# Sum-and-route stage with the shared expert: expert by batches with its weights stationary, positions behind each batch's logits

## The chip, the cores and the metric

The kernel is one launch on one NeuronCore of a Trainium2 chip. The metric is device time in microseconds (us), from the first to the last instruction of the core. TensorE (PE in the rows, PEld for its weight loads) multiplies, VectorE (DVE) and ScalarE (ACT) work element by element, GpSimd (POOL) issues the scatters by index, SyncE (SP) issues the other DMAs. Each engine runs its own list of instructions in order and waits for the others by semaphores.

## The reference

Four layers, each an attention or mixture (cond) and a feed-forward (ffn), on x of 4 batches of 512 tokens of 256 values, all in float32:

```python
x = x + _L0_ffn_ref(_L0_cond_ref(x, ...), ...)
x = x + _L1_ffn_ref(_L1_cond_ref(x, ...), ...)
x = x + _L2_ffn_ref(_L2_cond_ref(x, ...), ...)
x = x + _L3_ffn_ref(_L3_cond_ref(x, ...), ...)
```

The change lies where layer 1 ends and layer 2 begins. Layer 1 ends with a sum of two experts' rows per token; `_L2_cond_ref` is a mixture of 8 experts, of which each token takes two, plus one shared expert that all tokens take:

```python
logits = (logits_h + logits_g / GE_TEMP) / (1.0 + 1.0 / GE_TEMP)
topk_w, topk_idx = jax.lax.top_k(jax.nn.softmax(logits, axis=-1), K)   # K = 2 of E = 8
...
y = (y_sel * topk_w[..., None]).sum(1).reshape(b, s, h)
p = _leaky(hidden_states @ sw_gate) * (hidden_states @ sw_up) @ sw_down
y = y + p
```

`sw_gate`, `sw_up` and `sw_down` are 256x256 each; `_leaky` is max(x, 0.01 x).

## The kernel before

The program is a chain of stages (`stage`, line 89), each a block in which the five engines run their own lists, with a barrier between blocks: a stage starts when every engine has finished the one before. The stage of this case is `combine_and_share` (line 2312). Tokens lie 128 to a tile, 4 tiles to a batch, 16 tiles in all. Three things share the stage, each an object whose methods are called engine by engine, in an order written out by hand:

- `Combine` (`com`, L2216): VectorE adds the two weighted expert rows of a batch to `all_x`, eight instructions for a batch.
- `Router` (`part`): `tensor_turn` transposes the batch (L1655), ScalarE copies it to `all_xt` (L1620), `tensor` multiplies by the router's weights (L1670, L1674), `vector_ahead` takes the two largest of 8 logits for each token (L1717 to L1743), `tensor_after` counts with 0/1 matmuls how many earlier tokens chose each expert (L1687 to L1692, in bf16), `vector` makes the positions from these ranks (L1755 to L1761), and GpSimd scatters the batch's 8 tiles of rows, four of `all_x` and four of a copy (`scalar_double`, L1631), to the positions (L1605). `vector_last` (L1768 to L1799) makes the table of tiles and the routing weights. When all scatters have landed and the table is there, SyncE reads the table and loads the first tiles of sorted rows for the next stage (`first_rows`, L2006).
- `SharedExpert` (`shx`): tile by tile, in a pipeline. For tile t, `tensor(pe, t)` multiplies the tile (as the stationary side) with gate and up weights side by side (L2261, two matmuls of 512 columns into `gu_ps`), transposes the hidden values of tile t-1 (L2269, two), and multiplies those of tile t-2 with the down weights (L2277, two of 256 columns). ScalarE copies the gate half (L2286), the transposed hidden values (L2291) and the product to `all_h` (L2295); VectorE makes the leaky value (L2304) and the product with up (L2309).

The trace holds two records for each float32 matmul, so that "x4" beside L2261 is the two matmuls of one tile. After `part.tensor_after(pe, 3)` the PE list holds only the shared expert's tiles 7 to 15 and the two steps of tail; on VectorE `vector_last` stands behind tile 10.

Of the kernel before, what the change touches and what calls it, by code (L numbers as in the profile page):

```python
# [2231 lines left out]
class SharedExpert:  # L2232
# [6 lines left out]
    def __init__(self, nc, c, weights, com, stack):  # L2239
        m = Memory(nc, stack, "shx")  # L2240
        self.nc, self.c, self.com = nc, c, com
        self.wgu, self.wd, self.loaded = weights.wgu, weights.wd, weights.loaded
        self.act, self.lin, self.hid = ([m.sb(f"{x}{n}", [P, D]) for n in range(2)] for x in ("act", "lin", "hid"))
        self.hid_t = [m.sb(f"hid_t{n}", [P, KD, P]) for n in range(2)]
        self.gu_ps = [m.ps(f"gu_ps{n}", [P, 2, D]) for n in range(2)]
        self.t_ps = m.ps("t_ps", [P, KD, P])
        self.y_ps = m.ps("y_ps", [P, D])
        names = "gu_ready act_ready lin_ready hid_ready ht_ready ht_copied y_ready h_ready".split()
        (self.gu_ready, self.act_ready, self.lin_ready, self.hid_ready, self.ht_ready, self.ht_copied, self.y_ready,
         self.h_ready) = (m.sem(x) for x in names)  # L2250

    def tensor(self, pe, t):

        nc = self.nc
        if t == 0:
            pe.wait_ge(self.loaded, 48)
        if t < NT:
            if t >= 2:
                pe.wait_ge(self.hid_ready, t - 1)
            for k in range(KD):  # L2260
                last = nc.tensor.matmul(self.gu_ps[t % 2][:], self.c.xt[:, k, P * t:P * (t + 1)], self.wgu[:, k, :, :], start=(k == 0), stop=(k == KD - 1))  # L2261
            last.then_inc(self.gu_ready, 1)
        if 1 <= t <= NT:
            v = t - 1
            pe.wait_ge(self.hid_ready, v + 1)
            if v >= 1:
                pe.wait_ge(self.ht_copied, v)
            for f in range(KD):
                last = nc.tensor.transpose(self.t_ps[:, f, :], self.hid[v % 2][:, P * f:P * (f + 1)], self.c.ident[:])  # L2269
            last.then_inc(self.ht_ready, 1)  # L2270
        if t >= 2:
            v = t - 2
            pe.wait_ge(self.ht_copied, v + 1)
            if v >= 1:
                pe.wait_ge(self.h_ready, v)
            for f in range(KD):
                last = nc.tensor.matmul(self.y_ps[:], self.hid_t[v % 2][:, f, :], self.wd[:, f, :], start=(f == 0), stop=(f == KD - 1))  # L2277
            last.then_inc(self.y_ready, 1)

    def scalar(self, a, t):  # L2280
        nc = self.nc
        if t < NT:
            a.wait_ge(self.gu_ready, t + 1)
            if t >= 2:
                a.wait_ge(self.lin_ready, t - 1)
            nc.scalar.activation(self.act[t % 2][:], self.gu_ps[t % 2][:, 0, :], ACT.Copy).then_inc(self.act_ready, 1)  # L2286
        if 1 <= t <= NT:
            a.wait_ge(self.ht_ready, t)
            if t >= 3:
                a.wait_ge(self.y_ready, t - 2)  # L2290
            nc.scalar.activation(self.hid_t[(t - 1) % 2][:], self.t_ps[:], ACT.Copy).then_inc(self.ht_copied, 1)  # L2291
        if t >= 2:
            a.wait_ge(self.y_ready, t - 1)
            a.wait_ge(self.com.added, QT * ((t - 2) // QT + 1))
            nc.scalar.activation(self.c.h[:, t - 2, :], self.y_ps[:], ACT.Copy).then_inc(self.h_ready, 1)  # L2295

    def vector(self, dve, t):
        nc = self.nc
        if t < NT:
            n = t % 2  # L2300
# [388 lines left out]
```

## Time and profile before

| | us |
|---|---|
| median of three runs | 2277.09 (2274.95 to 2286.39) |
| the profiled execution | 2278.94 |
| its span on the core | 2277.1 |
| the stage: first to last instruction | 1157.86 to 1254.01 |

Busy time in the whole span: PE 2005.0 us (88%), DVE 1112.2 us (49%), ACT 988.5 us (43%), POOL 559.8 us (25%). The stage takes 96 of 2277 us. All rows below are of the profiled execution and count from its start. In a timeline row stand the start, the time taken, engine, line, operation and operands, the count, and in brackets how long the engine had been idle and what ended that; "remote" and "issue" mean that no instruction of another engine was found that the engine was waiting for at that moment. PEclk is the granted clock of TensorE, 1.00 for 2.4 GHz and 0.50 for 1.2 GHz.

### The profile page before, as it was taken

What the parts mean: (1) busy time and instruction counts of PE and PEld (TensorE: products, weight loads), DVE (VectorE), ACT (ScalarE), POOL (GpSimd) and SP (SyncE); (2) the same over time, 40 slices, a digit from 0 to 9 for tenths busy, and PEclk for the clock granted to TensorE, in tenths of its full rate; (3) what the DMA queues carried; (4) which work ended last, traced back from release to release, by engine and by line L of the source; (5) the groups of instructions that cost most, each with busy time, mean ns of one, the idle gap of its engine ahead of it and who ended that gap; (6) DMA issues with size and microseconds to landing.
All of it is one profiled execution on the core that took longest, in us unless ns stands there. A gap on an engine that the chain in (4) does not pass through costs nothing. (4 is left out here: it accounts for less than half of the span.)

```text
span 2277.1 us, 44630 instructions
## 1 busy us (share of the span) xinstructions
PE 2005.0 (88%) x15891; PEld 1415.1 (62%) x15891; DVE 1112.2 (49%) x3378; ACT 988.5 (43%) x2602; POOL 559.8 (25%) x872
## 2 busy tenths in 40 slices
PE   6899999897999996999967865996989999969994
PEld 3477777654777775566644544883567776736663
DVE  5388882275888824000043336006678883331113
ACT  2388881155888811111112231223678883212221
POOL 2022220065111115211123333115711111421111
PEclk9999999998999998999978986998989999979997
DMA  2185523001633121433131541741010004131113
GB/s 84 38 247 154 147 78 97 0 1 53 174 109 104 35 77 45 143 103 104 55 100 62 170 151 48 231 142 42 1 50 21 21 12 149 45 126 45 46 42 122
DMA packets 156826, 197.80 MB, mean 87 GB/s; under 512 B 15251, under 2 KB 129902, under 8 KB 156620
## 3 DMA queue, kind: packets, MB, share of 16 engines
q1 hardware_dynamic: 145004, 168.83, 24.6%
q0 software_dynamic: 11616, 26.26, 3.2%
q8 instruction: 124, 2.03, 0.4%
q14 instruction: 82, 0.67, 0.1%
HBM read 120.33 MB, written 88.64 MB: 92 GB/s over the span
## 5 line engine op out<-in xcount | busy, mean ns | idle before, releaser
L995 ACT ACTIVATE att_pr<-all_h,att_nmax 128x128 f32<-128x128 f32 (+3 forms) x768 | 420.8, 551 | 49.1 <-DVE att_nmax L948 49.1
L1059 PEld LDWEIGHTS att_t_ps<-all_ident,att_pr 64*128 64x128 f32 x3840 | 163.0, 139 | 104.0 <-issue 48.4
L1059 PE MATMUL att_t_ps<-all_ident,att_pr 64*128 64x64 f32 x3840 | 170.0, 223 | 10.4 <-DVE att_pt L957 10.3
L1255 PE MATMUL out_y_ps<-outw_wo,mem_qt 128*128 128x256 f32 x768 | 178.7, 386 | 0.0
L1918 PE MATMUL exp_f_h_ps<-exp_f_xs_t,cw_f_w 128*128 128x512 f32 (+1 forms) x512 | 172.7, 497 | 1.5 <-DVE exp_f_xs_t L1955 1.5
L1930 PE MATMUL exp_f_y_ps<-cw_f_w,exp_f_hid 128*128 128x256 f32 x768 | 168.4, 379 | 0.0
L957 DVE COPY att_pt<-att_t_ps 128x1024 f32<-128x1024 f32 (+2 forms) x168 | 166.7, 992 | 0.0
L1255 PEld LDWEIGHTS out_y_ps<-outw_wo,mem_qt 128*128 128x128 f32 x768 | 144.5, 193 | 24.7 <-issue 6.2
L1985 ACT ACTIVATE exp_f_hid<-exp_f_h_ps 128x512 f32<-128x512 f32 (+1 forms) x128 | 62.4, 490 | 219.3 <-PE exp_f_h_ps L1918 216.4
L1930 PEld LDWEIGHTS exp_f_y_ps<-cw_f_w,exp_f_hid 128*128 128x128 f32 x768 | 144.8, 190 | 19.5 <-issue 0.5
L995 ACT ACTIVATION_READ_ACCUMULATOR att_pr<-all_h,att_nmax 128x1 f32 x768 | 145.5, 189 | 0.0
L948 DVE CUSTOM_DVE_ANT_0 all_h<-att_s_ps,att_bias,mem3k_nsn 128x128 f32<-128x128 f32 (+3 forms) x256 | 128.2, 548 | 35.1 <-PE att_s_ps L1042 27.3
L948 DVE CUSTOM_DVE_ANT_0 all_h<-att_s_ps,att_bias,mem1k_nsn 128x128 f32<-128x128 f32 (+3 forms) x256 | 128.3, 549 | 34.8 <-PE att_s_ps L1042 26.2
L2100 PE MATMUL til_f_ab_ps<-tw_f_wab,til_f_xs_t 128*128 x312 | 143.4, 603 | 1.4 <-DVE til_f_xs_t L2161 1.4
L948 DVE CUSTOM_DVE_ANT_0 all_h<-att_s_ps,att_bias,mem0k_nsn 128x128 f32<-128x128 f32 (+3 forms) x256 | 127.9, 547 | 33.4 <-PE att_s_ps L1042 26.9
L1918 PEld LDWEIGHTS exp_f_h_ps<-exp_f_xs_t,cw_f_w 128*128 128x128 f32 x512 | 99.7, 195 | 68.8 <-issue 61.1
L915 POOL COPY att_rexp<-att_rinv 128x512 f32<-128x512 f32 x96 | 58.6, 610 | 336.5 <-DVE att_rinv L961 336.5
L1007 ACT ACTIVATE att_pt<-att_t_ps 128x1024 f32<-128x1024 f32 (+1 forms) x120 | 112.7, 939 | 39.9 <-PE att_t_ps L1059 35.7
L113 POOL TENSOR_TENSOR in_qn<-in_qn,all_minus_half 128x16 f32<-128x16 f32 x32 | 113.9, 3562 | 37.4 <-DVE in_qn L529 37.2
L730 PE MATMUL in_q_ps<-inw_wq,all_xt 128*128 128x512 f32 x256 | 119.9, 614 | 2.8 <-ACT all_xt L627 2.8
L1897 POOL DMA_INDIRECT expert_f<-exp_f_ys,exp_f_idx x48 | 46.7, 972 | 304.5 <-DVE exp_f_ys L1964 254.5
L2161 DVE COPY til_f_xs_t<-til_f_x_ps 128x256 f32<-128x256 f32 x39 | 16.6, 425 | 186.3 <-PE til_f_x_ps L2087 186.3
(395 smaller groups left out, 3661.6 us busy)
## 6 DMA issues: line engine op xcount, KB each, us to landing
sorted_c<-all_zero SPq DMA_DIRECT2D x8, 2056.0 KB, 14.1
sorted_f<-all_zero SPq DMA_DIRECT2D x8, 2056.0 KB, 11.8
cw_f_w<-in_L_ffn_w_dram SPq DMA_DIRECT2D x16, 1024.0 KB, 8.1
cw_f_w<-in_L_ffn_W_dram SPq DMA_DIRECT2D x16, 1024.0 KB, 7.0
band<-rev SPq DMA_DIRECT2D x2, 4096.0 KB, 19.3
att_bias<-band SPq DMA_DIRECT2D x32, 256.0 KB, 3.0
com_f_rows<-expert_f SPq DMA_DIRECT2D x16, 512.0 KB, 5.9
tw_f_wab<-in_L_ffn_w_dram SPq DMA_DIRECT2D x2, 4096.0 KB, 20.0
```

Source lines behind the costliest of these rows:

```text
L113: pool.tensor_tensor(value, value, c.minus_half[0:value.shape[0], 0:1].to_broadcast(list(value.shape)), ALU.pow).then_inc(ready, 1)
L730: last = nc.tensor.matmul(q_ps[t % 2][:, n, :], c.xt[:, k, P * t:P * (t + 1)], wq[:, k, S * n:S * (n + 1)], start=(k == 0), stop=(k == KD ...
L948: nc.vector.tensor_tensor_reduce(sc[u % 4][:, hh, at], s_ps[(2 * u + hh) % 3][:, at], bias_ap(i, q, hh), -1.0, c.nsn[:, b + k, q, h:h + 1] ...
L957: nc.vector.tensor_copy(*pt_and_turned(u)).then_inc(t_copied[e % 2], 1)
L995: nc.scalar.activation(pr[u % 4][:, hh, at], sc[u % 4][:, hh, at], ACT.Exp, scale=-1.0, bias=nmax[:, b + k, q, h:h + 1], accum_out=rsum[:, ...
L1007: nc.scalar.activation(*pt_and_turned(u), ACT.Copy).then_inc(t_copied[e % 2], 1)
L1059: last = nc.tensor.transpose(t_ps[e % 2][:, half, (q + 1) * (n * hh + k) + kb, :], pr[u % 4][d, hh, at:at + P], c.ident[d, d])
L1255: nc.tensor.matmul(y_ps[b % 2][:, q, :], c.out_t[:, p, P * at:P * (at + 1)], wo[:, p, :], start=(p == 0), stop=False)
L1918: last = nc.tensor.matmul(h_ps[f % 4][:, 0:cap], w1_sb[n][:, k, P * f:P * (f + 1)], xs_t[n][:, k, :], start=(k == 0), stop=(k == KD - 1))
L1930: last = nc.tensor.matmul(y_ps[(YT * n + t // 2) % 2][:, t % 2, :], hid[n][:, f, P * t:P * (t + 1)], w2_sb[n][:, f, :], start=(f == 0), st ...
L1985: nc.scalar.activation(hid[n][:, f, :], h_ps[f % 4][:, 0:cap], func).then_inc(hid_ready, 1)
L2100: last = nc.tensor.matmul(ab_ps[t % 2][:, n, :], xs_t[t % 2][:, k, :], tw.wab[:].rearrange("p (e k) n f -> p k n e f", k=KD)[:, k, n, at, ...
```

## The change

The router's and the combine's own instructions stay as they are; their places in the lists change. The shared expert is computed by batches of 512 tokens. The weights are now the stationary side and the tokens the moving one, so that the hidden values come out transposed, as the down product wants them: `tensor_gate(b, f)` makes half f of the hidden values of batch b, gate and up, in four matmuls of 512 columns; ScalarE copies the gate part and VectorE makes the two products, each on 512 columns; `tensor_out(b)` does the down product of the four tiles in eight matmuls of 256 columns, and `scalar_out` copies it to `all_h` in two pieces. The transposes (L2269) and their copies (L2291) are gone. Gate halves and outputs take turns in two PSUM buffers of two banks each.

```diff
-            for k in range(KD):
-                last = nc.tensor.matmul(self.gu_ps[t % 2][:], self.c.xt[:, k, P * t:P * (t + 1)], self.wgu[:, k, :, :], start=(k == 0), stop=(k == KD - 1))
...
-            for f in range(KD):
-                last = nc.tensor.transpose(self.t_ps[:, f, :], self.hid[v % 2][:, P * f:P * (f + 1)], self.c.ident[:])
...
+    def gate_bank(self, b, f):
+        return self.bank[(3 * b + f) % 2]
+    def out_bank(self, b):
+        return self.bank[(3 * b + 2) % 2].ap().rearrange("p a (t d) -> p a t d", d=D)
+    def tensor_gate(self, pe, b, f):
...
+        if b and f == 0:
+            pe.wait_ge(self.hid_ready, 2 * b)
+        if b and f == 1:
+            pe.wait_ge(self.h_ready, 2 * b)
+        for n in range(2):
             for k in range(KD):
+                last = nc.tensor.matmul(self.gate_bank(b, f)[:, n, :], self.wgu[:, k, n, P * f:P * (f + 1)], self.c.xt[:, k, S * b:S * (b + 1)],
+                                        start=(k == 0), stop=(k == KD - 1))
+        last.then_inc(self.gu_ready, 1)
+    def tensor_out(self, pe, b):
...
+        pe.wait_ge(self.hid_ready, 2 * b + 2)
+        for a in range(2):
+            for t in range(2):
+                tok = slice(P * (2 * a + t), P * (2 * a + t + 1))
+                for f in range(KD):
+                    last = nc.tensor.matmul(self.out_bank(b)[:, a, t, :], self.hid[b % 2][:, f, tok], self.wd[:, f, :], start=(f == 0), stop=(f == KD - 1))
             last.then_inc(self.y_ready, 1)
...
+    def scalar_gate(self, a, b, f):
...
+        self.nc.scalar.activation(self.act[n % 2][:], self.gate_bank(b, f)[:, 0, :], ACT.Copy).then_inc(self.act_ready, 1)
+    def scalar_out(self, a, b):
...
+            a.wait_ge(self.y_ready, 2 * b + n + 1)
+            self.nc.scalar.activation(self.c.h[:, QT * b + 2 * n:QT * b + 2 * n + 2, :], self.out_bank(b)[:, n, :, :], ACT.Copy).then_inc(self.h_ready, 1)
...
+        nc.vector.tensor_tensor(self.hid[b % 2][:, f, :], self.lin[n % 2][:], self.gate_bank(b, f)[:, 1, :], ALU.mult).then_inc(self.hid_ready, 1)
...
     @block.vector
     def _(dve):
         com.vector(dve, 0)
         com.vector(dve, 1)
         part.vector_ahead(dve, 0)
+        part.vector(dve, 0)
+        shx.vector_gate(dve, 0, 0)
         com.vector(dve, 2)
-        shx.vector(dve, 0)
-        part.vector(dve, 0)
         part.vector_ahead(dve, 1)
-        shx.vector(dve, 1)
+        part.vector(dve, 1)
+        shx.vector_gate(dve, 0, 1)
         com.vector(dve, 3)
...
         part.vector(dve, 3)
...
+        shx.vector_gate(dve, 2, 0)
+        shx.vector_gate(dve, 2, 1)
+        part.vector_last(dve)
+        shx.vector_gate(dve, 3, 0)
+        shx.vector_gate(dve, 3, 1)
```

On TensorE at the stage's start, from behind batch 1's transposes (before) and from batch 1's transposes (now); `turn_c` and `route_c` are the router's tiles, `shx` the shared expert's. Before:

```order
L1670 MATMUL turn_c_l_ps<-rw_c_wg_t,rw_c_g_t 128x32
L1674 MATMUL turn_c_l_ps<-rw_c_wr,all_xt 128x8 x8
L2261 MATMUL shx_gu_ps<-shw_wgu,all_xt 128x512 x2
L1687 MATMUL turn_c_r_ps<-route_c_sel,all_before 128x32
```

Now:

```order
L1655 MATMUL turn_c_x_ps<-all_ident,all_x 128x128 x8
L2268 MATMUL shx_bank<-all_xt,shw_wgu 128x512 x4
L1687 MATMUL turn_c_r_ps<-route_c_sel,all_before 128x32
L1692 MATMUL turn_c_r_ps<-route_c_sel,all_ones_b 128x24
L1692 MATMUL turn_c_r_ps<-route_c_sel,all_ones_b 128x16
L1692 MATMUL turn_c_r_ps<-route_c_sel,all_ones_b 128x8
L1670 MATMUL turn_c_l_ps<-rw_c_wg_t,rw_c_g_t 128x32
L1674 MATMUL turn_c_l_ps<-rw_c_wr,all_xt 128x8 x8
L2268 MATMUL shx_bank<-all_xt,shw_wgu 128x512 x4
```

The ranks of batch 0 (L1687, L1692) now stand ahead of batch 1's logits, behind one gate half.

On TensorE at the stage's end, the last two tiles' share of the list before:

```order
L2261 MATMUL shx_gu_ps<-shw_wgu,all_xt 128x512 x2
L2269 MATMUL shx_t_ps<-all_ident,shx_hid 128x128 x2
L2277 MATMUL shx_y_ps<-shw_wd,shx_hid_t 128x256 x2
L2269 MATMUL shx_t_ps<-all_ident,shx_hid 128x128 x2
```

and all that now stands behind the ranks of batch 3, for batches 2 and 3:

```order
L2268 MATMUL shx_bank<-all_xt,shw_wgu 128x512 x8
L2280 MATMUL shx_bank<-shw_wd,shx_hid 128x256 x8
L2268 MATMUL shx_bank<-all_xt,shw_wgu 128x512 x8
L2280 MATMUL shx_bank<-shw_wd,shx_hid 128x256 x8
```

Where each tile had its three short steps in turn, each of the two batches now has two gate halves and then its output in one block.

## Rows read from the trace of the kernel before

**Rows 1.** Stretches: length, PE, PEld, DVE, ACT, POOL busy, clock, DMA share, GB/s.

```profile
1177.80:1254.05 76.25, 59.36 (x229) 35.41 (x227) 34.09 (x127) 23.65 (x60) 31.75 (x32) 0.89 0.19 63
1222.00:1228.60 6.60, 3.83 (x8) 2.47 (x9) 0.85 (x2) 1.70 (x5) 1.95 (x2) 0.50 0.17 60
```

**Rows 2.** Timeline, PE, idle times inside the stage.

```profile
1207.23 0.44 PE L2269 MATMUL shx_t_ps<-all_ident,shx_hid 128*128 128x128 f32 x2 [2.74 <-DVE shx_hid L2309]
...
1216.25 1.10 PE L2277 MATMUL shx_y_ps<-shw_wd,shx_hid_t 128*128 128x256 f32 x4 [1.05 <-issue]
...
1222.58 0.66 PE L2269 MATMUL shx_t_ps<-all_ident,shx_hid 128*128 128x128 f32 x2 [3.51 <-issue]
1225.43 2.05 PE L2277 MATMUL shx_y_ps<-shw_wd,shx_hid_t 128*128 128x256 f32 x4 [2.19 <-issue]
...
1238.87 0.66 PE L2269 MATMUL shx_t_ps<-all_ident,shx_hid 128*128 128x128 f32 x2 [3.40 <-DVE shx_hid L2309]
```

**Rows 3.** Waits in 1157 to 1256: engine, line, releaser, us in total, times, longest.

```profile
ACT shx_act L2286 <- remote: 6.7, 3, 2.5
...
ACT shx_hid_t L2291 <- remote: 4.8, 2, 3.1
ACT all_h L2295 <- remote: 4.6, 3, 2.5
DVE route_c_slot L1755 <- DMA outw_ternary_w<-in_L_ffn_weight_dram: 4.5, 2, 2.9
```

**Rows 4.** Timeline, POOL, the first and the last of 32 scatters.

```profile
1180.88 1.02 POOL L1605 DMA_INDIRECT sorted_c<-all_x,r_c_pos  x1 [20.30 <-DVE r_c_pos L1761]
...
1223.53 0.98 POOL L1605 DMA_INDIRECT sorted_c<-turn_c_copy_rows,r_c_pos  x1 [0.30 <-issue]
```

**Rows 5.** Timeline, first and last operation of the table, and the load behind it.

```profile
1231.12 0.16 DVE L1768 COPY route_c_count<-turn_c_r_ps 128x8 f32<-128x8 f32 x1
...
1235.26 0.18 DVE L1786 CAST r_c_tile<-route_c_tile_n 128x39 int32<-128x39 f32 x1
...
1236.54 23.83 SPq L2006 DMA_DIRECT2D tw_c_xs<-sorted_c  x5
```

**Rows 6.** Timeline, PE, from batch 3's transposes to the ranks behind them.

```profile
1191.80 1.04 PE L1655 MATMUL turn_c_x_ps<-all_ident,all_x 128*128 128x128 f32 x8
1194.28 0.41 PE L1670 MATMUL turn_c_l_ps<-rw_c_wg_t,rw_c_g_t 64*128 64x32 f32 x2 [1.44 <-ACT all_xt L1620]
...
1196.42 1.96 PE L2261 MATMUL shx_gu_ps<-shw_wgu,all_xt 128*128 128x512 f32 x4
...
1198.44 1.03 PE L2277 MATMUL shx_y_ps<-shw_wd,shx_hid_t 128*128 128x256 f32 x4
1199.30 0.18 PE L1687 MATMUL turn_c_r_ps<-route_c_sel,all_before 128*128 128x32 bf16 x1
```

**Rows 7.** Timeline, tile 15: PE, ACT and VectorE, and PE's next transposes.

```profile
1247.29 1.88 PE L2261 MATMUL shx_gu_ps<-shw_wgu,all_xt 128*128 128x512 f32 x4
1249.01 0.38 PE L2269 MATMUL shx_t_ps<-all_ident,shx_hid 128*128 128x128 f32 x2
...
1250.56 0.44 PE L2269 MATMUL shx_t_ps<-all_ident,shx_hid 128*128 128x128 f32 x2 [0.30 <-DVE shx_hid L2309]
...
1249.21 0.38 ACT L2286 ACTIVATE shx_act<-shx_gu_ps 128x256 f32<-128x256 f32 x1 [1.33 <-PE shx_gu_ps L2261]
...
1249.63 0.42 DVE L2304 SCALAR_TENSOR_TENSOR shx_lin<-shx_act 128x256 f32<-128x256 f32 x1 [1.92 <-ACT shx_act L2286]
1250.09 0.42 DVE L2309 TENSOR_TENSOR shx_hid<-shx_lin,shx_gu_ps 128x256 f32<-128x256 f32 x1
```

**Rows 8.** Groups of the whole span: ACT and VectorE operations of 512 columns from PSUM.

```profile
L2142 ACT ACTIVATE til_f_act<-til_f_ab_ps 128x512 f32<-128x512 f32 x39 | 23.3, 597 | 106.2 <-PE til_f_ab_ps L2100 106.2
...
L2185 DVE TENSOR_TENSOR til_f_hid<-til_f_act,til_f_ab_ps 128x512 f32<-128x512 f32 x39 | 26.8, 688 | 5.1 <-ACT til_f_act L2142 5.1
```

**Rows 9.** Timeline, PE, batch 1's transposes.

```profile
1167.29 1.95 PE L1655 MATMUL turn_c_x_ps<-all_ident,all_x 128*128 128x128 f32 x8
```

More of the change, by code:

```diff
@@ L2249, in __init__ @@
-        (self.gu_ready, self.act_ready, self.lin_ready, self.hid_ready, self.ht_ready, self.ht_copied, self.y_ready,
-         self.h_ready) = (m.sem(x) for x in names)
-    def tensor(self, pe, t):
+        self.act, self.lin = ([m.sb(f"{x}{n}", [P, S]) for n in range(2)] for x in ("act", "lin"))
+        self.hid = [m.sb(f"hid{n}", [P, KD, S]) for n in range(2)]
+        self.bank = [m.ps(f"bank{n}", [P, 2, S]) for n in range(2)]
+        names = "gu_ready act_ready lin_ready hid_ready y_ready h_ready".split()
@@ L2335, in _ @@
         part.scalar_double(a, 0)
-        shx.scalar(a, 0)
-        shx.scalar(a, 1)
+        shx.scalar_gate(a, 0, 0)
+        shx.scalar_gate(a, 0, 1)
         part.scalar(a, 2)
         part.scalar_double(a, 1)
-        shx.scalar(a, 2)
-        shx.scalar(a, 3)
+        shx.scalar_out(a, 0)
+        shx.scalar_gate(a, 1, 0)
         part.scalar(a, 3)
         part.scalar_double(a, 2)
-        shx.scalar(a, 4)
-        shx.scalar(a, 5)
+        shx.scalar_gate(a, 1, 1)
+        shx.scalar_out(a, 1)
         part.scalar_double(a, 3)
-        shx.scalar(a, 6)
         part.scalar_last(a)
-        for t in range(7, NT + 2):
-            shx.scalar(a, t)
+        shx.scalar_gate(a, 2, 0)
+        shx.scalar_gate(a, 2, 1)
+        shx.scalar_out(a, 2)
+        shx.scalar_gate(a, 3, 0)
+        shx.scalar_gate(a, 3, 1)
+        shx.scalar_out(a, 3)
     @block.vector
@@ L2383, in _ @@
         part.tensor_turn(pe, 1)
+        shx.tensor_gate(pe, 0, 0)
+        part.tensor_after(pe, 0)
         part.tensor(pe, 1)
-        shx.tensor(pe, 0)
-        part.tensor_after(pe, 0)
-        shx.tensor(pe, 1)
+        shx.tensor_gate(pe, 0, 1)
         part.tensor_turn(pe, 2)
         part.tensor(pe, 2)
-        shx.tensor(pe, 2)
         part.tensor_after(pe, 1)
-        shx.tensor(pe, 3)
+        shx.tensor_out(pe, 0)
+        shx.tensor_gate(pe, 1, 0)
         part.tensor_turn(pe, 3)
         part.tensor(pe, 3)
-        shx.tensor(pe, 4)
         part.tensor_after(pe, 2)
-        shx.tensor(pe, 5)
-        shx.tensor(pe, 6)
+        shx.tensor_gate(pe, 1, 1)
+        shx.tensor_out(pe, 1)
         part.tensor_after(pe, 3)
-        for t in range(7, NT + 2):
-            shx.tensor(pe, t)
+        shx.tensor_gate(pe, 2, 0)
+        shx.tensor_gate(pe, 2, 1)
+        shx.tensor_out(pe, 2)
+        shx.tensor_gate(pe, 3, 0)
+        shx.tensor_gate(pe, 3, 1)
+        shx.tensor_out(pe, 3)
 def combine_and_relate(nc, c, com, part, rel, block):
```

83 lines of the change are left out of this document (21 added, 62 removed).

## The prediction

> **What bounds the kernel now.** The stages run one behind another, so the question is what ends this one, at 1254.0 in the profiled execution. I read the stage first by stretches [rows 1]: from 1177.8 to the end TensorE is busy for 59.4 of 76.3 us, and no other engine for more than 36. Then I followed the two strands that could end the stage. The scatters run from 1180.88 to 1224.5 [rows 4]; the table of tiles is done at 1235.44 and the first sorted rows are asked for 1.1 us later [rows 5], so this strand has some 10 us to spare. What ends last is the shared expert: tile by tile at 2.80 us (1.72 for gate and up, 0.22 for the transposes, 0.86 for the output) [rows 6, 7], on TensorE, which does nothing else behind batch 3's ranks.
>
> TensorE loses time in two ways. It stands idle: 2.74, 1.05, 3.51, 2.19 and 3.40 us are the idle times besides its short waits for the transposed batches [rows 2]. The last is VectorE's, which makes the table ahead of tile 11's hidden values. In the first four nothing was in the way: ScalarE started 8 small copies a total of 16.1 us after their inputs were there, and VectorE two rank reads 4.5 us late, with no releaser at that moment [rows 3]. All ten lie while GpSimd scatters or within 3 us of it. I call these late starts; I do not know their cause. The four idle times that they made add up to 9.5 us. And it runs slowly: a mean clock of 0.89 over 76.3 us means (1 - 0.89) x 2 x 76.3 = 16.8 us at 1.2 GHz; one such stretch of 6.6 us lies behind the idle times at 1222 and 1225 [rows 1, 2].
>
> **The change part by part.**
>
> *TensorE's work.* Gate and up cost the same columns as before: 32 matmuls of 512, and the outputs 32 of 256. A gate half is four of 512, 2 x 1.72 = 3.44 us at full clock; a batch's output is 4 x 0.86 = 3.44 us. The 32 transposes go: 16 x 0.22 = 3.5 us less. All of that was on the path.
>
> *The start.* Batch 1's transposes end at 1169.2, at half clock (1.95 us for what takes 1.04 later) [rows 6, 9]. Gate half (0,0) now follows at once: 6.9 us at half clock, to 1176.1. Then ranks of batch 0, 0.3 us, and batch 1's logits, over at about 1179.0 if the clock rises where it did (they take 2.14 at full clock [rows 6] and up to twice that at half).
>
> *The rest, at full clock.* Seven gate halves 24.1, four outputs 13.8, two batches of transposes 1.8, two of logits 2 x 2.14 = 4.3 [rows 6], ranks 0.5: 44.5 us, to 1223.5.
>
> *Waits of TensorE that stay or are new.* Logits of batches 2 and 3 wait for the copies of the transposed batch, 1.4 each [rows 6]: 2.8. The output of batch 0 waits for half (0,1) on VectorE, which comes behind batch 2's sum, logits and positions; walking VectorE's list gives 2.4. Outputs 1, 2 and 3 each stand directly behind their second gate half and wait for ScalarE and VectorE: for a tile of 256 columns this was 1249.01 to 1250.56, that is 1.55, of which 0.38 + 0.42 + 0.42 in the operations and 0.33 between them [rows 7]; at 512 columns the operations are 0.60, 0.69 and 0.69 [rows 8], so 2.3 us. Before, the next tile's gate matmuls stood in between and covered most of this; now nothing does. Three of 2.3: 6.9. Sum 12.1, to 1235.6, and the last copy 0.7: 1236.3.
>
> *What goes.* The 3.40 behind the table: `vector_last` now runs while TensorE does output 2 and half (3,0), 6.9 us, and VectorE's next work arrives 0.6 later still. All of the old stretch from 1231.12 to TensorE's restart at 1238.87 is 7.75 us with two tiles' products in it (1.7), so the cover is just enough; were it gone, up to 3.4 us come back, ahead of output 3.
>
> *The clock.* Not in this sum. The old list had 16.8 us at 1.2 GHz. The new one has fewer but regular idle times, of 2.3 and 2.4. I take four stretches of 3.3 us at half clock, 13.2 us, of which half is lost: 6.6. The bounds are 3.3 (two) and 16.5 (below). To 1242.9.
>
> *Late starts.* ScalarE's shared-expert list shrinks from 48 operations to 16, VectorE's from 32 to 16. If late starts fall on operations evenly, a third of 9.5 us stays on the path: 3.2. The bounds are 0, since none need fall on a copy that TensorE waits for, and 9.5. I take 3.2 because the copies are fewer and the output copies have 3 us of slack behind a gate half. To 1246.1.
>
> *Positions earlier.* Ranks of batch 0 are ready at 1176.4, the first scatter can start at about 1178.3 instead of 1180.88 [rows 4]. Batch 1 follows about 4 us earlier than before, batch 2 not much, and batch 3's ranks now stand behind output 1 (about 1213), in time for GpSimd, which then still scatters batch 2. I put the last scatter at 1219 to 1225. This is worth nothing: the table starts when half (2,1) is done, about when output 2 starts, 16.8 us ahead of the end (3.44 + 6.9 + 2.3 + 3.44 + 0.7), or 1229; 4.3 us later [rows 5] it is there, and the rows are asked for at 1235, with 11 us to spare.
>
> *ScalarE and VectorE.* They save 32 + 16 operations; both are idle more than half of the stretch [rows 1], so it counts only in the waits above.
>
> **The sum.** 1246.1 against 1254.0 is 8 us less. Nothing behind the stage changes. The profiled execution took 2278.94, so 2271; against the median, 2277.09 - 8 = 2269.
>
> **Rivals.**
>
> *Clean.* The late starts were a matter of many small copies and vanish; two stretches at half clock remain: 1236.3 + 3.3 = 1239.6, 14 us less, 2263. For it: 17 operations instead of 48. Against it: VectorE's two late starts were on lone rank reads [rows 3], of which there are as many now.
>
> *No gain.* What the expert gains in work it loses in lock-step: late starts cost the full 9.5 on the shorter list too, since each now holds up a whole batch: 1242.9 + 9.5 = 1252.4, 1.6 less, 2275.5. For it: eight of ten late starts came in the second half of the scatters, where outputs 1 and 2 now wait for lone copies.
>
> *Slower by the clock.* Each of the four long waits is followed by 6.6 us at 1.2 GHz, as that at 1222 was [rows 1], and the two short ones by 3.3: 4 x 3.3 + 2 x 1.65 = 16.5 us lost; with 9.5 of late starts the stage ends at 1236.3 + 26.0 = 1262.3, 8 us later, 2285. It decides from 17.7 us of both together. For it: the transposes behind the idle times of 3.51 and 3.40 took 0.66 us, where 0.38 is the time at full clock [rows 2, 7]. Against it: behind the 1.44 the outputs took 0.86 as ever [rows 6], and behind the 2.74 the transposes took 0.44; 2.3 lies between. [...]
>
> *The scatters end the stage.* If GpSimd gets positions late (batch 3's behind output 1), the last scatter moves past 1225; it would have to move past about 1240 to count. I give this nothing of its own.
>
> **How the numbers follow.** Forecast 2269 with its own range 2265 to 2273: 0.48. Clean, 2263: 0.25. No gain, 2275.5: 0.18. Slower, 2285: 0.09. Half a per cent is 11.4 us, about what a measurement of this kernel can tell from no change. Faster by more than that means under 2265.7: clean, nearly whole, and a little of the forecast, 0.28. Slower by more means over 2288.5: 0.03. The rest, 0.69, is within. The range reaches from the lower edge of clean (1236.3, 2259.5) to short of the slower case: 2260 to 2281.
>
> **What would show it.** In the profile of the changed kernel: the stage ends 8 us earlier relative to its start; gate halves at 3.44 us; TensorE idle for 2.3 ahead of outputs 1, 2 and 3 and for about 2.4 ahead of output 0; no wait of TensorE for the table; first scatter within 3 us of half (0,0)'s end; the load of sorted rows some 10 us ahead of the end; clock about 0.88 behind batch 1's logits. The prediction is wrong if late starts on ScalarE sum to over 10 us on the path or to none, if the clock lies at 0.5 through whole output blocks, or if the load of rows ends the stage.

## The result, and the profile after

The changed kernel takes 2272.9 us (median of 20 runs, 2268.8 to 2280.7), the kernel before, in 20 runs on the same chip, 2283.3 (2275.0 to 2293.1). The ratio is 0.9951, with a 95% interval of 0.9940 to 0.9962: 10 to 11 us less. The profiled execution has a span of 2267.7 us against 2277.1.

The stretches of the stage, from its first matmul to the end of its last copy (us, then PE, PEld, DVE, ACT, POOL busy with counts, clock, DMA share, GB/s); first the kernel before, whose row in [rows 1] begins later:

```profile
1157.80:1254.05 96.25, 75.01 (x286) 47.81 (x286) 46.90 (x167) 27.04 (x67) 34.27 (x43) 0.81 0.22 73
```

and the kernel after:

```profile
1160.60:1243.70 83.10, 65.04 (x254) 43.11 (x254) 45.02 (x151) 19.84 (x35) 34.83 (x43) 0.84 0.25 84
```

The stage is 13.2 us shorter. TensorE's busy time fell by 10.0 (transposes and clock), its idle time from 21.2 to 18.1 us. It began 2.8 us later than before, from work ahead of it that the change does not touch, so the stage's end moved by 10.4 us; the span moved by 9.4. PE's timeline after, with the idle time ahead of each row in brackets; these answer to [rows 2, 6, 9]:

```profile
1170.07 1.95 PE L1655 MATMUL turn_c_x_ps<-all_ident,all_x 128*128 128x128 f32 x8
1171.81 4.43 PE L2268 MATMUL shx_bank<-all_xt,shw_wgu 128*128 128x512 f32 x8
...
1176.59 1.95 PE L1674 MATMUL turn_c_l_ps<-rw_c_wr,all_xt 128*128 128x8 f32 x16
...
1184.13 0.40 PE L1670 MATMUL turn_c_l_ps<-rw_c_wg_t,rw_c_g_t 64*128 64x32 f32 x2 [1.18 <-ACT all_xt L1620]
...
1191.97 6.37 PE L2280 MATMUL shx_bank<-shw_wd,shx_hid 128*128 128x256 f32 x16 [5.44 <-DVE shx_hid L2310]
1198.18 3.60 PE L2268 MATMUL shx_bank<-all_xt,shw_wgu 128*128 128x512 f32 x8
...
1211.91 3.72 PE L2280 MATMUL shx_bank<-shw_wd,shx_hid 128*128 128x256 f32 x16 [2.13 <-DVE shx_hid L2310]
...
1224.87 3.72 PE L2280 MATMUL shx_bank<-shw_wd,shx_hid 128*128 128x256 f32 x16 [2.13 <-DVE shx_hid L2310]
...
1237.59 5.41 PE L2280 MATMUL shx_bank<-shw_wd,shx_hid 128*128 128x256 f32 x16 [2.13 <-DVE shx_hid L2310]
1243.93 0.41 PE L2087 MATMUL til_c_x_ps<-all_ident,tw_c_xs 128*128 128x128 f32 x2 [0.94 <-PEq L92]
```

L2268 is a gate half, L2280 an output. A block at full clock takes 3.6 to 3.7 here; 4.43, 6.37 and 5.41 ran in part at 1.2 GHz. The four idle times ahead of outputs are the hand-offs. The wait of 3.40 for the table [rows 2] is gone. Two late starts are left that matter, one on each engine (the second just hidden behind a gate half); they answer to [rows 3]:

```profile
1189.69 0.19 DVE L1755 TENSOR_TENSOR route_c_slot<-turn_c_r_ps,route_c_base 128x32 f32<-128x32 f32 x1 [4.22 <-remote]
...
1190.51 0.68 DVE L2305 SCALAR_TENSOR_TENSOR shx_lin<-shx_act 128x512 f32<-128x512 f32 x1
1191.23 0.69 DVE L2310 TENSOR_TENSOR shx_hid<-shx_lin,shx_bank 128x512 f32<-128x512 f32 x1
...
1230.97 0.60 ACT L2296 ACTIVATE all_h<-shx_bank 128x512 f32<-128x512 f32 x1 [2.29 <-remote]
```

The ranks were ready at 1186.5, VectorE read them at 1189.7, and the products that output 0 waits for stand behind: 3.2 us of the 5.44. The first scatter comes at 1178.1, the load of sorted rows at 1231.8, 12 us ahead of the end.

### The profile page after: what moved, and what is told of

Read it like the earlier page. It is cut to its first block and busy times, and to the rows that moved or that the text cites. A ratio compares the mean times of both kernels' runs of the same rounds, so it can differ in the third digit from the quotient of the medians.

```text
span 2267.7 us, 44437 instructions
## 1 busy us (share of the span) xinstructions
PE 1994.7 (88%) x15859; PEld 1408.3 (62%) x15859; DVE 1110.3 (49%) x3362; ACT 981.8 (43%) x2570; POOL 561.6 (25%) x872
## 5 line engine op out<-in xcount | busy, mean ns | idle before, releaser
L1059 PE MATMUL att_t_ps<-all_ident,att_pr 64*128 64x64 f32 x3840 | 169.7, 223 | 10.7 <-DVE att_pt L957 10.6
## 6 DMA issues: line engine op xcount, KB each, us to landing
sorted_c<-all_zero SPq DMA_DIRECT2D x8, 2056.0 KB, 14.4
```

Source lines behind the costliest of these rows:

```text
L1059: last = nc.tensor.transpose(t_ps[e % 2][:, half, (q + 1) * (n * hh + k) + kb, :], pr[u % 4][d, hh, at:at + P], c.ident[d, d])
```

## The experiments

The theory that I took into them: the new form of the expert makes the gain (fewer transposes, fewer small copies that can start late), the earlier positions make none. The rival: the order makes part of it.

### Each part alone

Only the new expert, with positions in the old place:

```
         com.vector(dve, 1)
         part.vector_ahead(dve, 0)
-        part.vector(dve, 0)
-        shx.vector_gate(dve, 0, 0)
         com.vector(dve, 2)
+        shx.vector_gate(dve, 0, 0)
+        part.vector(dve, 0)
...
         part.tensor_turn(pe, 1)
+        part.tensor(pe, 1)
         shx.tensor_gate(pe, 0, 0)
         part.tensor_after(pe, 0)
-        part.tensor(pe, 1)
```

> The new shared expert by batches, but the router's steps of batch 0 and 1 in the old order: batch 1's logits ahead of the first gate half and of batch 0's ranks on TensorE; on VectorE batch 2's sum ahead of batch 0's positions, and batch 1's positions behind half (0,1) and batch 3's sum. Theory: the gain is the expert's form, not the earlier positions, so nearly all of it is here: 9 to 12 us less than before (0.995 to 0.996). It may even win 1 to 3 us more than the whole change, since half (0,1)'s products no longer stand behind batch 1's rank read, which came 3 us late in the changed kernel. Rival (the earlier positions pay): 0 to 5 us less than before. The first scatter should come at about 20 to 23 us after the stage's start instead of 17.4.

Only the order, with the expert by tiles as before:

```
         part.vector_ahead(dve, 0)
+        part.vector(dve, 0)
+        shx.vector(dve, 0)
         com.vector(dve, 2)
...
         part.tensor_turn(pe, 1)
+        shx.tensor(pe, 0)
+        part.tensor_after(pe, 0)
         part.tensor(pe, 1)
```

> The old shared expert tile by tile, with each batch's ranks and positions directly behind its logits, as in the change. Theory: scatters start 2 to 3 us earlier, the expert still ends the stage with its short steps, its late starts and the wait for the table, so within 2 us of before, either way. Rival (the earlier positions pay): 5 us or more less than before.

Measured, on a second chip, against 2269.6 us for the kernel before in 23 runs: the new expert alone 2272.2, ratio 1.0007 (0.9993 to 1.0021); the order alone 2272.1, ratio 1.0001 (0.9983 to 1.0019). So my theory missed for the expert: alone it was to gain 9 to 12 us and gained nothing; its first scatter came 26.4 us into the stage, not 20 to 23. The order alone came out within its 2 us, but not with the late starts that were expected to stay. For the kernel before was itself 14 us faster here than on the chip of the first measurement. In both traces not one copy or product of the stage started late, with the same 32 scatters beside them. The stage took 81.35 us with the new expert in the old order (1161.00 to 1242.35) and 85.5 us with the new order and the expert by tiles (1165.00 to 1250.50), against 96.3 for the kernel before on the first chip. Both left the first comparison without a base: it had to be made again with both kernels on one chip.

### The scatters taken away

In both kernels GpSimd was made to wait for the expert's last copy before it scatters (the same work, in another order).

```
         part.pool_first(pool)
+        pool.wait_ge(shx.h_ready, 16)
         for b in range(B):
             part.pool(pool, b)
```

> The kernel before with all 32 scatters held back until the shared expert's last copy; nothing else changed. The time as a whole grows by 40 us or so and says nothing; what counts is the time from the stage's first instruction to the expert's last copy, 96.1 us before. Theory (the late starts come from scatters running beside the other engines): ScalarE's and VectorE's waits without a releaser (20.6 us in 10) all but vanish, TensorE's idle times of 2.74, 1.05, 3.51 and 2.19 fall below 0.6 each, and the stretch is 82 to 86 us. Rival (they belong to the lists, to many small copies with two waits each): they stay, and the stretch is 94 to 97 us.

> The changed kernel with all 32 scatters held back until the shared expert's last copy. Stretch from the stage's first instruction to the expert's last copy: 82.9 us with the scatters beside it. Theory (late starts come from the scatters): TensorE's idle time ahead of output 0 falls from 5.44 to 2.3 or so, output 0 may then run at full clock, and the stretch is 77 to 80 us. Rival (late starts belong to the lists): 82 to 84 us.

Measured, one run each on the chip of the last two: 2312.9 and 2325.8 us. TensorE then waits 49 us for the next stage, in the first and in the second:

```profile
1287.77 0.66 PE L2087 MATMUL til_c_x_ps<-all_ident,tw_c_xs 128*128 128x128 f32 x2 [48.90 <-PEq L92]
```

```profile
1292.15 0.66 PE L2087 MATMUL til_c_x_ps<-all_ident,tw_c_xs 128*128 128x128 f32 x2 [49.13 <-PEq L92]
```

Held back, the scatters stand in line behind the expert, and the kernels take 43 and 56 us more than the kernel before, so beside the expert is where they belong. Their own question stayed unanswered. The old expert's list, from 1157.2 to its last copy's end at 1239.3, took 82.1 us without scatters, and the new one's, from 1163.8 to 1243.7, 79.9; both lie in the range of the theory, but on this chip nothing started late with scatters either.

### Both kernels again, on one chip

> The kernel before, unchanged, for a profile beside the next three. In the profile of before, ScalarE and VectorE started late ten times in the stage and TensorE lost 9.5 us to it; the two one-part kernels, profiled on another chip, show no late start at all, with the same 32 scatters. If late starts come with the chip or the hour and not with the old form of the expert, this profile has none where the others of this call have none, and the stage (first matmul of the stage to the first of the next) takes 86 to 88 us in place of 96.4. If they come with the old form (its 104 short copies and products), they are here again and the stage takes 94 to 97 us.

> The changed kernel, unchanged, beside the kernel before on the same chip. If the late starts come with the chip: on a chip without them the stage takes 80 to 82 us, the change is worth 5 to 6 us in the stage, part of which the start of the last expert stage takes back (its load of weights came 3.4 us late in place of 0.9 with the new expert alone), and the ratio is 0.997 to 1.000; on a chip with them 0.994 to 0.996 as measured first. If the change itself removes them, 0.994 to 0.996 on either.

Measured on a third chip: before 2271.6 us (29 runs), changed 2267.9 (12 runs), ratio 0.9989 (0.9978 to 1.0000). The same two programs that were 10.4 us apart are 2.5 apart by the ratio, and 3.7 by the medians. The stretch of the stage, before and after:

```profile
1164.10:1246.40 82.30, 70.75 (x286) 45.99 (x286) 47.11 (x167) 27.41 (x67) 34.72 (x43) 0.84 0.26 85
```

```profile
1163.20:1243.10 79.90, 64.97 (x254) 43.07 (x254) 44.95 (x151) 19.88 (x35) 34.83 (x43) 0.86 0.26 86
```

That is 2.4 us less, where the first chip had 13.2. The rows say where the rest was. From the first chip to this one the kernel before became 13.9 us shorter here: 9.7 of idle time (21.2 to 11.6) and 4.3 of busy time, which is clock. The changed kernel became 3.2 shorter: 3.1 of idle time and 0.1 of busy time. Neither trace has a late start. How far the 2.4 can be trusted other traces without late starts tell: on the second chip, without scatters, the difference was 2.2 (82.1 and 79.9), and on the fourth, from two kernels below that differ from these only 750 us later, it was 4.6:

```profile
1161.70:1246.40 84.70, 73.13 (x286) 47.67 (x286) 47.13 (x167) 27.44 (x67) 34.18 (x43) 0.81 0.25 83
```

```profile
1161.25:1241.35 80.10, 65.16 (x254) 43.19 (x254) 44.94 (x151) 19.83 (x35) 34.84 (x43) 0.85 0.26 87
```

The new form's stage takes 79.9 to 80.1 in all three. The old one's takes 82.1 to 84.7, and what varies is its busy time, so the low clock. The change itself is thus worth 2.2 to 4.6 us in the stage. In TensorE's timeline of the kernel before, the idle times of 2.74, 1.05, 3.51 and 2.19 [rows 2] have no counterpart; only the wait for the table is there:

```profile
1225.82 1.88 PE L2261 MATMUL shx_gu_ps<-shw_wgu,all_xt 128*128 128x512 f32 x4
1231.15 0.44 PE L2269 MATMUL shx_t_ps<-all_ident,shx_hid 128*128 128x128 f32 x2 [3.45 <-DVE shx_hid L2309]
```

and in the changed kernel output 0 waits 2.35 in place of 5.44:

```profile
1191.47 6.24 PE L2280 MATMUL shx_bank<-shw_wd,shx_hid 128*128 128x256 f32 x16 [2.35 <-DVE shx_hid L2310]
```

So late starts come with the chip (or its hour), not with the form of the expert; the form decides only how much of them lies on the path. The first branch of both expectations held, but for the sizes in the stage: the kernel before took 82.3 us and not 86 to 88, and the change was worth 2.4 and not 5 to 6.

### What the new form pays: the hand-offs

Two more kernels, on the chip of the last two. In the first, outputs 1 to 3 go to the router's two banks of transposed rows, which are free by then, so that a gate half can stand ahead of outputs 1 and 2; it also has the edit of the second kernel.

```
     def gate_bank(self, b, f):
-        return self.bank[(3 * b + f) % 2]
+        return self.bank[f if b == 0 else (f + 1) % 2]
-    def out_bank(self, b):
-        return self.bank[(3 * b + 2) % 2].ap().rearrange("p a (t d) -> p a t d", d=D)
+    def out_bank(self, b, a):
+        whole = self.part.x_ps[a] if b else self.bank[0][:, a, :]
+        return whole.rearrange("p (t d) -> p t d", d=D)
...
         part.tensor_after(pe, 2)
         shx.tensor_gate(pe, 1, 1)
-        shx.tensor_out(pe, 1)
-        part.tensor_after(pe, 3)
         shx.tensor_gate(pe, 2, 0)
+        part.tensor_after(pe, 3)
+        shx.tensor_out(pe, 1)
         shx.tensor_gate(pe, 2, 1)
-        shx.tensor_out(pe, 2)
         shx.tensor_gate(pe, 3, 0)
+        shx.tensor_out(pe, 2)
         shx.tensor_gate(pe, 3, 1)
         shx.tensor_out(pe, 3)
```

> The changed kernel, with outputs 1 to 3 written to the two banks of the router's transposed rows, free by then, so that a gate half stands ahead of outputs 1 and 2, and with VectorE's products of the second half ahead of the choice of batch 1. Theory: the hand-offs are the price of the new form: two of 2.13 us go and so does the wait ahead of output 0 (5.4 us with a late start, about 2 without), 6 to 8 us less than the changed kernel in this call; the stage takes 73 to 77 us. Rival: VectorE, with the router's table between the products, or the load of sorted rows behind the last scatter sets the end then, and under 2 us are won.

The second has only VectorE's order changed:

```
         com.vector(dve, 2)
+        shx.vector_gate(dve, 0, 1)
         part.vector_ahead(dve, 1)
         part.vector(dve, 1)
-        shx.vector_gate(dve, 0, 1)
```

> The changed kernel with one edit: VectorE makes the products of half (0, 1) ahead of batch 1's choice and positions, not behind them. Theory: output 0 waited for these products because they stand behind a rank that comes later; the wait ahead of output 0 falls from 2 us (5.4 with the late start) to under 0.5, and the stage is 2 to 3 us shorter than the changed kernel's. Rival: the positions and so the scatters of batch 1 come 1.4 us later and the late start lies elsewhere, so that it is within 1 us.

Measured: outputs in the router's banks 2262.1 us, ratio to before 0.9960 (0.9948 to 0.9972), 5.8 us under the changed kernel; VectorE's order alone 2267.0, ratio 0.9985 (0.9971 to 0.9999), 0.9 under it. The stretches of the first and of the second:

```profile
1161.65:1235.85 74.20, 64.59 (x254) 42.16 (x254) 44.68 (x151) 19.87 (x35) 35.15 (x43) 0.86 0.27 92
```

```profile
1161.70:1242.50 80.80, 67.47 (x254) 44.33 (x254) 44.76 (x151) 19.85 (x35) 35.03 (x43) 0.83 0.26 86
```

The first is nearly what its theory said: a stage of 74.2 us (73 to 77 expected), 5.7 us shorter than the changed kernel's, nearly all of it idle time (14.9 to 9.6), and 5.8 us in the whole time, where 6 to 8 were expected. In TensorE's timeline the waits ahead of outputs 0 and 1 are gone, that ahead of output 2 is 0.55, that ahead of output 3 stays:

```profile
1210.99 3.70 PE L2285 MATMUL turn_c_x_ps<-shw_wd,shx_hid 128*128 128x256 f32 x16
...
1222.11 3.72 PE L2285 MATMUL turn_c_x_ps<-shw_wd,shx_hid 128*128 128x256 f32 x16 [0.55 <-DVE shx_hid L2315]
...
1231.39 3.72 PE L2285 MATMUL turn_c_x_ps<-shw_wd,shx_hid 128*128 128x256 f32 x16 [2.13 <-DVE shx_hid L2315]
```

The second missed. Output 0 no longer waits, idle time fell by 1.6 us, but busy time rose by 2.5, because other blocks now lay at the low clock:

```profile
1201.60 5.38 PE L2268 MATMUL shx_bank<-all_xt,shw_wgu 128*128 128x512 f32 x8
1209.11 5.34 PE L2280 MATMUL shx_bank<-shw_wd,shx_hid 128*128 128x256 f32 x16 [2.13 <-DVE shx_hid L2310]
```

One wait taken away, with three as long left, bought nothing that can be measured (the stage took 0.9 us more, the whole time 0.9 less); with three of the four gone or short, the stage won 5.7.

### A second place: the load of the last expert stage

The 2.4 us of the stage do not arrive at the end of that pair of traces: the spans are 2266.8 before and 2268.9 changed. And the new expert alone gained nothing. (By 12 and 29 runs the changed kernel is the faster by 2.5 in spite of it, so single traces differ by more than is explained here.) The place is 750 us later, in code that nobody changed. From the first matmul of the last expert stage to the end takes 263.4 us in the kernel before (the second trace of it) and 267.8 in the changed one. The wait there, before:

```profile
2004.65 6.41 PE L2100 MATMUL til_f_ab_ps<-tw_f_wab,til_f_xs_t 128*128 x8 [0.61 <-DVE til_f_xs_t L2161]
...
2021.30 1.99 PE L2117 MATMUL til_f_y_ps<-twd_f_wd,til_f_hid_t 128*128 x8 [0.98 <-DMA twd_f_wd<-in_L_ffn_w_dram]
```

and changed:

```profile
2002.39 5.26 PE L2100 MATMUL til_f_ab_ps<-tw_f_wab,til_f_xs_t 128*128 x8 [0.61 <-DVE til_f_xs_t L2161]
...
2020.44 3.77 PE L2117 MATMUL til_f_y_ps<-twd_f_wd,til_f_hid_t 128*128 x8 [3.54 <-DMA twd_f_wd<-in_L_ffn_w_dram]
```

TensorE comes to the wait 1.15 us sooner after that stage's first matmul, the load lands later after its issue, and behind the longer wait TensorE runs at 1.2 GHz (3.77 for 1.99). All five traces of kernels with the new expert so far, other than that of the first chip, have it: the load takes 15.6 to 15.9 us, against 14.4 to 14.5 with the old expert. The DMA view of the load's time, changed kernel (queue, packets, MB, share):

```profile
q1 hardware_dynamic: 4564, 4.60, 90.9%
q8 instruction: 1, 0.02, 0.7%
q14 instruction: 1, 0.01, 0.1%
```

With the kernel before, q1 stands there alone. The new form has fewer instructions, so fetches of code fall elsewhere. To test this I put the missing number back as instructions that do nothing, at the head of that stage:

```
+            if mx.name == "f3":
+                for _ in range(188):
+                    pe.wait_ge(tw.loaded, 32)
             turn_x(0)
```

Two of these waits make one instruction: the trace of this kernel has 194 instructions more than the changed one's, 94 of them on TensorE and the others on ScalarE (66) and VectorE (34), whose lists have such a loop too.

> The changed kernel, with instructions that do nothing (waits already met) at the head of the last expert stage, in the 12 us in which its engines are idle: 94 on TensorE, 66 on ScalarE, 34 on VectorE, which is what the new form has fewer, so that the program behind them lies where it lay in the kernel before. In the five profiles of kernels with the new expert, on two chips other than the first, the load of twd_f_wd there lands after 15.6 to 15.9 us, one 16 KB instruction packet and one of 8 KB fall into it, TensorE waits 3.4 us for it and goes on at half clock; with the old expert none falls into it, it lands after 14.4 to 14.5 us, and the wait is 0.9 to 1.0. Theory: the place of the fetches does it; the load lands after 14.5 us, the wait is at most 2.2, from there to the end takes 263.5 to 265.5 us in place of 267.7, and the kernel is 2 to 4 us faster than the changed one beside the same before (ratio about 0.997). Rival: something else of the new form delays the load, and nothing changes.

> The kernel with outputs in the router's banks (stage 74.4 us, ratio 0.9960) with the same instructions that do nothing at the head of the last expert stage. Theory: both gains stand side by side, 2 to 4 us more, ratio 0.9940 to 0.9955. Rival: the padding is worth nothing, ratio 0.996.

> The reverse: the kernel before, with 162, 190 and 222 instructions that do nothing on TensorE, ScalarE and VectorE at the same place, each 256 less the number above, so that with 16 KB (256 instructions) to a fetch the fetches behind it fall where they fall in the changed kernel. Theory: the load of twd_f_wd lands after 15.6 to 15.9 us with an instruction packet in it, the wait rises from 1.0 to 2.2 us or more, and the kernel is 1 to 4 us slower than before (ratio 1.0005 to 1.002). Rival: no packet in the load, wait and time as before, within 1 us. Its stage of the shared expert is a third look at late starts: none, and 82 to 86 us, if this chip has none.

Measured on a fourth chip, where the kernel before took 2272.0 us: 2275.2 for the changed kernel with fillers, ratio 1.0026 (1.0011 to 1.0041); 2270.0 with outputs in the router's banks and fillers, 0.9993 (0.9983 to 1.0004); 2289.4 for the kernel before with fillers, 1.0084 (1.0069 to 1.0100). All three missed, for a reason of their own making: fillers are not free. TensorE's idle time ahead of that stage rose from some 12 us to 22 in the first:

```profile
2010.16 0.66 PE L2087 MATMUL til_f_x_ps<-all_ident,all_zero 128*128 128x128 f32 x2 [22.29 <-issue]
```

which is 10 us for 94 of them, 0.1 us each. As the stage began that much later than its load was issued, the load was long there, and its wait was gone in all three. What can be read is the load by itself: it landed after 15.0 and 14.8 us in the first two, with no instruction packet in it. In the third it took 14.8 us with three of 8 KB but none of 16 KB in it; so the small ones hardly matter, and the reverse, a 16 KB packet put into the old kernel's load, did not come about. No late starts in any of the three.

The last kernel, that with outputs in the router's banks, has 32 fillers where TensorE is idle for 22.6 us anyway:

```
     @block.tensor
     def _(pe):
+        for _ in range(64):
+            pe.wait_ge(part.loaded, part.rw.all_loaded)
         part.tensor_second(pe)
```

> The kernel with outputs in the router's banks (ratio 0.9960 in its call) with 32 instructions on TensorE that do nothing, this time at the head of the stage behind the tiles of the small experts, where TensorE is idle for 22.6 us: the 94 fillers of the last call lay on the path and cost about 10 us (TensorE's idle time ahead of the last expert stage went from 12.3 to 22.3 us), which hid what they were to show. 32 fillers at 0.107 us each are 3.4 us, inside the idle time. Theory: TensorE's 16 KB fetch, which came 4.7 us into the last expert stage and into the load of twd_f_wd, comes ahead of it; the load lands after at most 15 us in place of 15.6, TensorE's wait of 3.4 us falls to 2.2 or less, the time from that stage's first matmul to the end falls from 267.4 to 263 to 265.5 us, and the ratio is 0.994 to 0.9955. Rival: the load lands as late without the packet, or the 8 KB packet alone delays it: wait 3.4, 267 us, ratio 0.996.

It ran on another chip, called the fifth here, and that was of the first kind (it may even be the first, whose number is not on record): the kernel before took 2285.1 us (11 runs), this one 2272.4 (6 runs), ratio 0.9942 (0.9922 to 0.9962), within the expected range, but not for the reason given. The 16 KB packet did come ahead of the load's issue, TensorE's wait for the load was 1.67 us, and from that stage's start to the end took 264.7. But the first products took 6.77 us there and not 5.26, so TensorE also came later to the wait, as in the changed kernel on the first chip (6.32, then a wait of 1.89). The question stays open: in the traces that tell its landing, the load takes 0.6 to 1.5 us more with the 16 KB packet than without; but the long wait also needs TensorE to be early, and no run separated the two.

There is a second candidate, which none of these runs was built to test. SyncE's timeline, before and changed:

```profile
2006.55 0.44 SPq L2057 DMA_DIRECT2D twd_f_wd<-in_L_ffn_w_dram  x1
...
2021.63 7.39 SPq L2006 DMA_DIRECT2D twd_f_xs<-sorted_f  x2
```

```profile
2004.31 0.44 SPq L2057 DMA_DIRECT2D twd_f_wd<-in_L_ffn_w_dram  x1
...
2018.22 0.33 SPq L2006 DMA_DIRECT2D twd_f_xs<-sorted_f  x1
```

Where TensorE is early, the next sorted rows (`twd_f_xs`) are also asked for sooner. In the five traces with the long wait their load of 128.5 KB is issued 13.8 to 14.0 us after that of `twd_f_wd`, and so while it runs; in the four with the old expert and no fillers 15.1 to 15.2 us after it, when it has landed. No trace has the 16 KB packet in the load without these rows. In the two traces of the new form on chips of the first kind they come 14.9 us after it, without the packet, and TensorE's wait ends 15.5 and 15.3 us after the issue, where it ends after 14.7 to 14.8 with the old expert. By their size neither explains it: at the 350 GB/s that the load runs at, 128.5 KB are an estimated 0.4 us and 16 KB 0.05, of 1.1 to 1.5. What makes TensorE early there (5.26 for the first products in place of 6.41) is open too.

The run answered the other question. The late starts are back, in a kernel whose form without fillers had none on the third chip. Waits of the whole span in this run:

```profile
DVE route_f_lg L1717 <- remote: 12.3, 1, 12.3
...
ACT shx_act L2294 <- remote: 8.7, 2, 7.8
DVE route_c_slot L1755 <- remote: 6.0, 2, 4.1
ACT all_h L2301 <- remote: 5.6, 1, 5.6
```

One of them holds up TensorE for 8.3 us, ahead of output 2; ScalarE's row and TensorE's:

```profile
1230.83 0.60 ACT L2294 ACTIVATE shx_act<-shx_bank 128x512 f32<-128x512 f32 x1 [7.83 <-remote]
```

```profile
1232.99 5.39 PE L2285 MATMUL turn_c_x_ps<-shw_wd,shx_hid 128*128 128x256 f32 x16 [8.28 <-DVE shx_hid L2315]
```

Its stage took 82.4 us, 8.2 more than on the third chip. The 32 scatters ran from 1183.2 to 1230.1 in it, and the late copy started 0.7 us after the last of them. The first of these rows is of a second stage with scatters, 750 us later. Most of its 12.3 us is an ordinary wait, but VectorE starts 1.0 us after TensorE's logits are there (1.0 and 2.3 in the two traces of the first chip, 0.04 in that of the kernel before on the third). In all: three traces on the chips where the kernel before takes 2283 to 2285 us have late starts of ScalarE and VectorE in this stage, and eleven on the three where it takes 2270 to 2272 have none, nor such a row in the second stage.

## Why the prediction was right, point by point

2269 was forecast and 2272.9 measured, 8 us less and 10.4. The range held, and the likeliest case was the right one in its mechanism: fewer late starts on the path, four hand-offs, a part of the low clock. That the number is this close is partly luck. The stage itself became 13.2 us shorter, not 8, which is nearer to the clean case's 14; in the trace 2.8 us of it are hidden by the later start of the stage and 1.0 by what lies behind it. And the forecast was worked from a median of three runs, 2277.1, where 20 runs gave 2283.3. By its own steps:

- **TensorE's work.** 3.44 for a half and for an output; measured, from start to start, 3.4 to 3.6. The 32 transposes went. The matmuls, taken one by one, add up to some 1.5 us more than the 44.5 of the sum.
- **The start** was the mis-sized term. Half (0,0) was put at 6.9 us at half clock and took 4.3; logits of batch 1 took 1.95 at full clock. They were over 17.7 us into the stage and not 21.1: 3.4 us better. The step "if the clock rises where it did" failed. Before, TensorE stood idle 1.2 us between the transposes of batch 1 and its logits, and these still took 3.58; now the half fills that gap, and the clock was up before it was over. All nine traces in which the expert's matmuls stand there have 1.95 for these logits, and all five in which the logits stand there, the expert alone among them, 3.58. That the gap does it is argued: the kind of matmuls changed with it.
- **Waits that stay.** Logits of batches 2 and 3 waited 1.18 each (1.4 forecast), hand-offs 2.13 three times (2.3), output 0 2.35 where nothing started late (2.4). The walk through VectorE's list and the sum 0.60 + 0.69 + 0.69 plus what lies between was good to 0.2 us.
- **The wait for the table** went, as forecast.
- **"Nothing behind the stage changes"** failed. The last expert stage, 750 us later, took 263.4 us to the end before and 264.5 after on the first chip, and 267.4 to 267.8 in the five traces of the new expert on the second and third.
- **Clock.** 6.6 forecast, in four stretches. Output 0 took 2.65 us more than output 1, output 3 took 1.7 more: 4.3. The bounds held. Behind batch 1's logits the mean clock was 0.90 (0.88 forecast).
- **Late starts.** 3.2 forecast on the path, 3.1 measured (5.44 ahead of output 0 against 2.35 on the third chip). The size was right, and the reasoning behind it only in part: I let them fall by the number of operations. ScalarE's two did lie where they cost little; VectorE's lone rank read was the one on the path, which I had named as what speaks against the clean case. With the same number of operations the run on the fifth chip lost 8.3 us to one of them. So 3.2 was a fair middle, and one trace does not confirm the rule.
- **Positions earlier: worth nothing.** Right for the scatters: 12 us of slack at the end. The order alone measured 1.0001; what its earlier clock gave, later stretches at 1.2 GHz took back (75.2 us busy in its stage, against 70.7 and 73.1 for the old order without late starts).
- **Two counts and a reading were off.** The clean case speaks of 17 operations of ScalarE, of which the list has 16, and the no-gain case puts eight of ten late starts into the second half of the scatters, where seven are. Neither is in the sum. For VectorE's two rank reads [rows 3] name a load of weights as releaser, not none; in the program the read waits only for TensorE's ranks (`rank_ready`), so it was a late start all the same.
- **What the profile after was to show** (12 us ahead of the end, first scatter within 3 us, no wait for the table) it showed.

*The rivals.* In "clean" the stage takes 1239.6 - 1157.9 = 81.7 us; the changed kernel's takes 79.9 on the third chip. But the case was priced as a gain of 14 us, on the ground that the late starts were a matter of many small copies. Where they are absent they are absent from the kernel before too, and the gain is 2.2 to 4.6 in the stage. "No gain" and "slower by the clock" did not come. The Trainium skill ("TensorE: Matmul & The Clock Gate", section "HAM oscillation") describes a kernel whose bursts are each shorter than the wait behind them, and in which every burst starts at the low clock. Here TensorE works for 10.6 and 10.8 us between its waits of 2.13, so the page's case is not this one, and the rows lie between it and no effect: behind the same wait of 2.13, outputs 1 and 2 of the changed kernel took 3.72 (full clock) and output 3 took 5.41; with VectorE's order changed, output 1 took 5.34 behind it. A wait of 2.13 may cost up to 1.7 us more, and need not.

*What the prediction did not ask* is whether the 9.7 us of idle time and the 4.3 of clock behind them, 13.9 us of a stage of 96.3, belonged to the kernel. It took them as given, said that their cause was not known, and let the change save two thirds of them. On this chip that is what happened: of the 13.2 us in the stage, 10.8 are late starts and their clock (13.9 less the changed kernel's 3.2), and 2.4 are the change; with the old form's spread in clock, 8.6 to 11.0 and 2.2 to 4.6. What a late start is stays unknown. On chips that do not have them the whole change measured 0.1% (0.0 to 0.2).

## What to carry to other kernels

Before a wait is priced, look at whether something in the kernel makes it: idle time with no releaser inside the program may belong to the chip, and then the gain of a change that avoids it holds only there. Measure both kernels on a second chip before calling such a gain the change's own.

A form with fewer, larger blocks pays for each hand-off in full unless another block stands ahead of it: look for banks that fall free in the middle of a stage. Here two of them were worth 5.8 us, more than the change itself where nothing starts late, and their gain came from several waits together; with one alone taken away, the low clock lay elsewhere and ate the gain.

## What the runs showed of the hardware

- Late starts of ScalarE and VectorE, with idle times of up to 7.8 us ahead of them, appear on the first and the fifth chip (perhaps one and the same), in three different programs, and on the other three chips in none of eleven traces. In all three traces they lie while GpSimd scatters or within 3 us behind. The scatters are no sufficient cause, as the same 32 have none elsewhere; whether they are needed for it could not be tried, as the run without scatters beside the expert fell on a chip without late starts.
- With a block of the expert's matmuls in the idle time of 1.2 us between two blocks at half clock, the clock rose sooner, in nine traces of nine; whether the filled gap or the kind of matmuls does it was not separated. Stretches of the kernel before, 12.1 to 19.1 us into the stage, and after, 13.3 to 17.7 us into it (the clock is the third number from the end):

```profile
1170.00:1177.00 7.00, 6.59 (x21) 5.08 (x22) 4.02 (x13) 1.40 (x3) 0.00 (x0) 0.50 0.00 0
```

```profile
1174.00:1178.40 4.40, 4.40 (x29) 3.05 (x27) 1.90 (x6) 0.78 (x3) 0.29 (x1) 1.00 0.00 0
```

- An instruction that does nothing but wait for what is there costs TensorE 0.1 us, so 94 of them cost 10 us. Kernels with other instruction counts also fetch code at other times, 750 us away from the edit; whether that delays a load there, or the rows that are loaded beside it, stays open.
